# A fused attention and expert kernel: the round's products in pieces of 32 weight columns, and another order of two transfers and a store

## What is computed

```python
q, k, v = split_heads(x @ Wq), split_heads(x @ Wk), split_heads(x @ Wv)      # 16 heads of 8
attn = softmax(einsum('bhqd,bhkd->bhqk', q, k) * e ** -0.5) + bias[None]
x = _layernorm(x + _layernorm_eps3(einsum('bhqk,bhkd->bhqd', attn, v)) * gamma + beta)
sim = (x @ hasher_w.T) @ keys.T
vals, idx = top_k(sim, 4); w = softmax(vals)
for k in range(4):
    out += (silu(x @ values_down[idx[k]]) @ values_up[idx[k]]) * w[k]
x = _layernorm(x + (x + out * scale))
```

## Time and profile before

| | us |
|---|---|
| median of 3 runs | 327.17 |
| lowest and highest | 325.89, 327.17 |
| the profiled execution's own time | 326.0 |
| its span in the profile | 324.2 |

### The profile page before, as it was taken

How to read it: one execution, slowest core, us unless ns; L and a number is a source line. 1 busy time by engine, 2 the same in 40 slices (tenths; PEclk the granted TensorE clock), 3 DMA queues, 4 the chain that set the end, 5 groups by cost and what they waited for, 6 DMA issues and landing times.

```text
span 324.2 us, 4925 instructions
## 1 busy us (share of the span) xinstructions
PE 296.1 (91%) x1633; PEld 125.3 (39%) x1658; DVE 233.2 (72%) x516; ACT 200.5 (62%) x392; POOL 125.7 (39%) x209
## 2 busy tenths in 40 slices
PE   4778979999999989999999999996999999999991
PEld 2544322223232233333544533332455433275481
DVE  4548778788879869987778699873876763156673
ACT  3675366685767567788655577884646689911610
POOL 8492700110104641146466111493275022963133
PEclk9999999999999999999999999997999999999998
DMA  5486593279520203020202020024000000100002
GB/s 164 109 248 162 132 328 88 62 273 305 156 74 4 74 2 77 2 73 4 73 4 73 4 74 3 1 66 116 0 4 0 4 3 1 34 0 2 0 0 65
DMA packets 28246, 23.17 MB, mean 71 GB/s; under 512 B 6542, under 2 KB 26686, under 8 KB 28222
## 3 DMA queue, kind: packets, MB, share of 16 engines
q1 hardware_dynamic: 27950, 22.73, 24.7%
q10 hardware_dynamic: 272, 0.13, 0.1%
HBM read 12.18 MB, written 10.52 MB: 70 GB/s over the span
## 4 chain that ended last, share of the span: by engine, by line
PE 71%; DVE 10%; ACT 6%; DMA 4%; POOL 3%; issue 3%; SPq 1%; POOLq 0%; DVEq 0%
PE sm_ps L1136 18%; PE ov_ps L1165 16%; PE st_ps L1147 12%; DVE neg_max L830 6%; PE si_ps L1183 6%; PE mi_ps L1259 5%; ACT probs L705 3%; PE mi_ps L1171 2%; PE st_ps L1388 2%; DMA q_stack<-shift_rows 2%; DMA k_stack<-stack_dram 1%; PE si_ps L1189 1%; PE mi_ps L1244 1%; PE si_ps L1264 1%; PE st_ps L1189 1%
## 5 line engine op out<-in xcount | busy, mean ns | idle before, releaser
L830 DVE TENSOR_REDUCE neg_max<-sm_ps 128x1 f32<-128x512 f32 x256 | 167.3, 686 | 48.7 <-PE sm_ps L1136 47.5
L705 ACT ACTIVATE probs<-st_ps 128x512 f32<-128x512 f32 x256 | 137.5, 606 | 47.2 <-PE st_ps L1147 39.4
L1136 PE MATMUL sm_ps<-k_stack,q_stack 96*128 96x512 bf16 x256 | 98.5, 386 | 5.7 <-DVE neg_max L830 2.4
L1147 PE MATMUL st_ps<-q_stack,k_stack 128*128 128x512 bf16 x232 | 78.5, 382 | 3.9 <-DMA q_stack<-shift_rows 2.5
L1165 PE MATMUL ov_ps<-probs,v_cur 128*32 128x512 f32 x512 | 69.1, 611 | 0.0
L1136 PEld LDWEIGHTS sm_ps<-k_stack,q_stack 96*128 96x128 bf16 x256 | 24.7, 97 | 94.4 <-DVE neg_max L830 76.3
L472 POOL TENSOR_TENSOR hid<-hid,w_rows 128x512 f32<-128x512 f32 x26 | 32.7, 1274 | 38.3 <-ACT w_rows L616 38.2
L1147 PEld LDWEIGHTS st_ps<-q_stack,k_stack 128*128 128x128 bf16 x256 | 25.0, 99 | 29.7 <-ACT probs L705 8.2
L893 DVE SCALAR_TENSOR_TENSOR hid<-tanh_sb,mi_ps 128x512 f32<-128x512 f32 x24 | 16.3, 681 | 12.3 <-ACT tanh_sb L742 12.3
L1259 PE MATMUL mi_ps<-x_t,down_sb 128*128 128x512 f32 x48 | 24.5, 591 | 0.2 <-ACT probs L705 0.2
L1183 PE MATMUL si_ps<-up_sb,hid 128*128 128x128 f32 x192 | 24.3, 275 | 0.0
(11 more groups left out here) (162 smaller groups left out, 296.8 us busy)
## 6 DMA issues: line engine op xcount, KB each, us to landing
stack_dram<-parts SPq DMA_DIRECT2D x18, 384.0 KB, 4.5
q_stack<-stack_dram SPq DMA_DIRECT2D x16, 288.0 KB
k_stack<-stack_dram SPq DMA_DIRECT2D x16, 288.0 KB
stack_dram<-parts SPq DMA_DIRECT2D x6, 288.0 KB, 4.4
x_sb<-L_attn_x SPq DMA_DIRECT2D x4, 256.0 KB, 3.2
out<-y_out SPq DMA_DIRECT2D x3, 256.0 KB, 2.3
stack_dram<-parts SPq DMA_DIRECT2D x6, 96.0 KB, 2.1
down_sb<-L_ffn_values_down SPq DMA_DIRECT2D x1, 512.0 KB, 8.2
```

The costliest lines, as they stand in the source:

```text
L705: nc.scalar.activation(probs[:, u % 2, j, :], st_ps[:, score_bank(u * J + j), :], ACT.Exp, scale=SCORE_SCALE).then_inc(probs_ready, 1)
L830: nc.vector.tensor_reduce(neg_max[:, g % 2, col:col + 1], sm_ps[:, c % 2, :], AX.X, ALU.max, negate=True).then_inc(max_ready, 1)
L1136: nc.tensor.matmul(sm_ps[:, c % 2, :], q_stack[0:SHIFT_ROW, h, c * P:(c + 1) * P], k_stack[0:SHIFT_ROW, h, :], start=True, stop=True).then ...
L1147: nc.tensor.matmul(st_ps[:, score_bank(k), :], k_stack[:, g * J + j, kc * P:(kc + 1) * P], q_stack[:, g * J + j, :], start=True, stop=True ...
```

## The change

`tiled` makes one product as separate matmuls, each with 32 of the weight columns and the whole moving operand, into the quarters of 32 partitions of the same bank; `tiled_turn` does the same for a bf16 transpose, `whole` is the product as it was. Scores, maxima, both expert layers, `sim`, the spreads, and the bf16 turns (`shift`, `wt`) of the rounds go through them. Whole as before are: the set-up, the maxima made in it, the f32 transposes (`o0`, `o1`, `x1t`), and in the tail the spreads, the first layer and the last `up`. The tail's eight `up` of the sequence before the last use the same function `up` as the rounds, and so are in pieces too. In SyncE's queue `load_shift(t + 1, 0)` now stands ahead of `load_slice(t + 1, 2)`, and `store(t - 2)` behind both. The rest of the diff gives names to places and tables that hold the same places as before.

```diff
--- before.py
+++ after.py
@@ -393,14 +401,14 @@
                     load_slice(t + 1, 1)
                 if attention:
                     load_shift(t, 3)
-                if late:
-                    store(t - 2)
                 if is0(t):
                     for b in range(3, B):
                         write_parts(b, slice(0, H), parts_written[b])
                 if attention and more:
+                    load_shift(t + 1, 0)
                     load_slice(t + 1, 2)
-                    load_shift(t + 1, 0)
+                if late:
+                    store(t - 2)
 
             def store(f):
 
@@ -1124,7 +1133,23 @@
                                          wv_sb[:], start=True, stop=True)
                 i.then_inc(prep_mm, 1)
 
-            def maximum_scores(t, pos, c):
+            def tiled(dst, weights, moving, **flags):
+
+                for n in range(weights.shape[-1] // TILE):
+                    i = nc.tensor.matmul(dst[n * TILE:(n + 1) * TILE], weights[:, n * TILE:(n + 1) * TILE], moving,
+                                         **flags)
+                return i
+
+            def tiled_turn(dst, src, idn):
+
+                for n in range(src.shape[-1] // TILE):
+                    i = nc.tensor.transpose(dst[n * TILE:(n + 1) * TILE], src[:, n * TILE:(n + 1) * TILE], idn)
+                return i
+
+            def whole(dst, weights, moving, **flags):
+                return nc.tensor.matmul(dst, weights, moving, **flags)
+
+            def maximum_scores(t, pos, c, product=tiled):
 
                 n, h = t * U + pos, pos % U
                 k = C * n + c
@@ -1133,8 +1158,8 @@
                 if not (is0(t) and pos == 0 and c < 2):
 
                     pe.wait_ge(max_ready, k - 1)
-                nc.tensor.matmul(sm_ps[:, c % 2, :], q_stack[0:SHIFT_ROW, h, c * P:(c + 1) * P],
-                                 k_stack[0:SHIFT_ROW, h, :], start=True, stop=True).then_inc(sm_ready, 1)
+                product(sm_ps[:, c % 2, :], q_stack[0:SHIFT_ROW, h, c * P:(c + 1) * P], k_stack[0:SHIFT_ROW, h, :],
+                        start=True, stop=True).then_inc(sm_ready, 1)
 
             def scores(t, u, j):
 
@@ -1144,9 +1169,8 @@
                 if not (is0(t) and k < 3):
 
                     pe.wait_ge(probs_ready, J * n + j + 1 - scores_since(k))
-                nc.tensor.matmul(st_ps[:, score_bank(k), :],
-                                 k_stack[:, g * J + j, kc * P:(kc + 1) * P],
-                                 q_stack[:, g * J + j, :], start=True, stop=True).then_inc(scores_ready, 1)
+                tiled(st_ps[:, score_bank(k), :], k_stack[:, g * J + j, kc * P:(kc + 1) * P],
+                      q_stack[:, g * J + j, :], start=True, stop=True).then_inc(scores_ready, 1)
 
             def values(t, u):
 
@@ -1180,8 +1204,8 @@
                         pe.wait_ge(side_done, count)
                 pe.wait_ge(weighed, hidden_count(f, j))
                 for c in range(C):
-                    i = nc.tensor.matmul(si_ps[:, c * P:(c + 1) * P], hid[:, j, c * P:(c + 1) * P], up_sb[:, j, :],
-                                         start=(j == 0 and c == 0), stop=(j == FJ - 1), skip_group_check=True)
+                    i = tiled(si_ps[:, c * P:(c + 1) * P], hid[:, j, c * P:(c + 1) * P], up_sb[:, j, :],
+                              start=(j == 0 and c == 0), stop=(j == FJ - 1), skip_group_check=True)
                 if j == FJ - 1:
                     i.then_inc(side_ready, 1)
 
@@ -1229,7 +1253,7 @@
                 elif name.startswith("shift"):
                     g = int(name[5:])
                     pe.wait_ge(shift_split, (t + 1 if g == 0 else t) * G + g + 1)
-                    i = turn(mi_bf[:, 0:P], shift_parts[:].rearrange("p i n -> p (i n)"), ident_bf[:])
+                    i = tiled_turn(mi_bf[:, 0:P], shift_parts[:].rearrange("p i n -> p (i n)"), ident_bf[:])
                 elif name == "x1t":
                     if t < B:
                         pe.wait_ge(pool_step, pool_at(f, "bscale"))
@@ -1241,14 +1265,14 @@
 
                     pe.wait_ge(misc_done, job(t, "x1t", is_kept))
                     for c in range(C):
-                        i = nc.tensor.matmul(bank[:, c * NE:(c + 1) * NE], x1_t[:, c * P:(c + 1) * P], sim_w[:],
-                                             start=True, stop=True)
+                        i = tiled(bank[:, c * NE:(c + 1) * NE], x1_t[:, c * P:(c + 1) * P], sim_w[:],
+                                  start=True, stop=True)
                 elif name == "wt":
                     pe.wait_ge(w_split, f + 1)
                     pe.wait_ge(spread_made, PARTS)
                     for c in range(C):
-                        i = turn(si_bf[0:PARTS * NE, c * P:(c + 1) * P], w_parts[:, c].rearrange("p i n -> p (i n)"),
-                                 ident_bf[:])
+                        i = tiled_turn(si_bf[0:PARTS * NE, c * P:(c + 1) * P],
+                                       w_parts[:, c].rearrange("p i n -> p (i n)"), ident_bf[:])
                 elif name in SPREAD:
                     pe.wait_ge(side_done, job(t, "wt", is_side))
                     i = spread_weights(bank[:, :], int(name[1:]))
@@ -1256,12 +1280,12 @@
                     j = int(name[4:])
                     if j == 0:
                         pe.wait_ge(experts_loaded, 32)
-                    i = nc.tensor.matmul(mi_ps[:], down_sb[:, j * NJ:(j + 1) * NJ, :], x1_t[:],
-                                         start=True, stop=True)
+                    i = tiled(mi_ps[:], down_sb[:, j * NJ:(j + 1) * NJ, :].rearrange("k n d -> k (n d)"), x1_t[:],
+                              start=True, stop=True)
                 i.then_inc(ready, 1)
 
-            def spread_weights(bank, j):
-                return nc.tensor.matmul(bank, spread[:, j].rearrange("r n p -> r (n p)"), w_t[:], start=True, stop=True)
+            def spread_weights(bank, j, product=tiled):
+                return product(bank, spread[:, j].rearrange("r n p -> r (n p)"), w_t[:], start=True, stop=True)
 
             early = [divmod(k, C) for k in range(EARLY)]
 
@@ -1269,7 +1293,7 @@
 
                 for _ in range(n):
                     if early and EARLY - len(early) < most:
-                        maximum_scores(0, *early.pop(0))
+                        maximum_scores(0, *early.pop(0), product=whole)
 
             for b in range(B):
                 prep(b)
@@ -1382,7 +1406,7 @@
                     nc.tensor.matmul(bank, ident_bf[:], k_stack[:, 0, :], start=True, stop=True)
 
             def tail_spreading(j):
-                spread_weights(tail_bank(j), j).then_inc(tail_spread, 1)
+                spread_weights(tail_bank(j), j, product=whole).then_inc(tail_spread, 1)
 
             def tail_first_layer(j):
                 nc.tensor.matmul(tail_down_bank(j), down_sb[:, j * NJ:(j + 1) * NJ, :], x1_t[:],
```

## The result

| | before | after |
|---|---|---|
| median us | 327.17 (4 runs) | 312.98 (4 runs) |
| lowest and highest | 325.89, 327.39 | 312.77, 313.24 |
| profiled execution, its span | 326.0, 324.2 | 312.77, 311.0 |

The ratio is 0.9574, 95% interval 0.9549 to 0.9600: faster by 14 us by the medians, by 13.2 between the two profiled executions. 324.2 was forecast. The time lies at rival 1 (311.7), which had a chance of 0.20; the range held it.

A forecast was written before the change was run, and what follows sets the result against it. TensorE was taken to bound most of rounds 2 and 3, ScalarE the last window. Queue -4.3 and shape +2.5 sum to -1.8 us, from the profiled 326.0 to 324.2 us; range 311.5 to 335.

The forecast's parts named there:

- rival 1: Tiles cost nothing over a whole product: a plain unit takes 2.64 instead of 2.85; 311.7 us in all, chance 0.20.
- What bounds the kernel: TensorE in round 2 and first half of round 3, ScalarE in the last window, a two-engine loop in round 0.
- Part 1, the queue: End of round 2: shift rows issued ahead of slice and store close the 2.7 us hole and its low clock, -4.3 us.
- Part 2: The shape, 32-column pieces in rounds and tail: -2.6 + 2.2 + 1.5 + 1.4 = +2.5 us.
- Price of a product of 32-column weights: A product in 32-column pieces takes 0.24 us instead of 0.22, so a plain unit changes by -0.03.
- A smaller step: In round 2, small transposes and `sim` together were to cost 0.3 us.
- Rival 3: Four times the pairs make instructions the bound, 0.06 us a pair, in rounds and tail: +11.8, 338 us, chance 0.20.
- The rule weighed: Each further tile adds about 4 ns: a product would take 0.23, the shape about 3 us less in rounds 1 to 3.

## Why the prediction was wrong

- **What bounds the kernel: right.** TensorE in most of the rounds, VectorE in round 0, ScalarE at the end of round 3, a hole of 2.7 us with its low clock.
- **Part 1, the queue: right.** -4.3 forecast; -4.2 by the spans of the queue-alone run, 4.3 by its round 2. That it is worth 6.2 once the shape is changed was not seen: the forecast simply added the two.
- **Part 2, the failing step: "Price of a product of 32-column weights", 0.24 instead of 0.22.** It measures 0.22. The 0.02 came from the values' second pass, 0.45 behind the first instead of 0.43. That pass stood right behind a change of shape, and the excess is a part of it: with the same shape ahead, the values step 0.43. The prediction asked whether the excess was special to f32, and not whether it was special to the place behind a change. The one misread row went into a plain unit twice: as 8 x 0.02 lost by the products in pieces, and as 2 x 0.02 that the values' two passes were not expected to get back. These 0.20 us are the difference between the forecast -0.03 a unit and the measured -0.23.
- **What hangs on that step.** Round 0: -2.6 forecast, -2.6 measured, and that is luck. The forecast had each of 16 units go from 3.09 to 2.93. In the trace 13 units lose 0.21 to 0.22 (3.09 becomes 2.87, rival 1's figure), two stay, and the one with the f32 transposes, which stay whole, is 0.18 longer. Round 1: 0, measured -2.0. Round 2, shape alone: +2.2, measured 62.7 - 69.2 + 4.3 = -2.2. Round 3: +1.5, measured -1.6. Tail: +1.4, measured -0.3: its 256 pairs of `up` take 7.20 us, row below, against 7.31. Rounds and tail together, the shape is worth about -8.7 on top of the queue's -4.3; +2.5 was forecast.
- **A smaller step.** `sim` was forecast to cost (in the 0.3 for small transposes and sim) and took 0.5 us less each time, up to 2 us in all.
- **Rival 1: right, and nearly in size.** -3.5, -2.6, -2.8, -1.3 by rounds; measured -2.6, -2.0, -2.2, -1.6. It gave rounds 0 and 1 too much, since it let every unit gain, and in part of them something else than TensorE sets the pace. That its total of -14.3 is so near the 13.2 has some luck in it: it had neither the 1.9 us by which queue and shape help each other nor what `sim` saves.
- **Rival 3, instructions as the bound: wrong.** It needed 0.033 us a pair in the tail; measured are 0.027, after TensorE's timeline in the tail:

```profile
273.49 7.20 PE L1139 MATMUL si_ps<-up_sb,hid 128*32 128x128 f32 x256
```

  (7.20 - 0.27) / 255 = 0.027, held for 7 us; the 32 pairs of `sim` behind it go at 0.012 each (284.52 to 284.91, rows in the last section). It was priced from one instruction behind an idle stretch; the burst of eight in the same rows, 0.16 us, was the better witness.
- **The rule weighed.** The Trainium skill ("TensorE: Matmul & The Clock Gate", Part 3, The mechanism) has about 4 ns for each further tile. From the first to the fourth start within a score it is 10 ns in the median of the kernel after, 3 to 4 ns each, so the figure fits, but it isn't paid per product: each quarter is started again 0.22 us after its last start, and the step from product to product stays at 0.22. Behind a change of shape, as at the values before, it is 20 ns. Two starts this close also lie well under the 25 ns between starts that the prediction set beside rival 3. The same page of the Trainium skill, section "Wait — 56ns, not 53.3ns?", has about 62 ns of sequencer time for a matmul without the hardware decode; an estimate by it for the tail's 256 matmuls is 15.9 us, and the row above has 7.20, so that path was not the one taken.

What stays open is what the 0.10 us of a change consists of. The traces show that loads aren't made ahead over it, and that the next product's first load starts some 0.10 us after the 0.22 of the product ahead (158.17 to 158.49 above); whether that is a drain of the array, a part of the load, or both, was not varied by itself. Open too is what `sim` in pieces is worth by itself.

## What to carry to other kernels

Count the changes of tile shape between neighbouring products, not the instructions: each costs 0.10 us or more, so one small product of another shape in every unit is paid 64 times, and it can pay to cut everything else to its shape. Do it for all or for none: with two thirds or one third of the products cut, this kernel was slower than with none. And when a price is read from a row, ask what stands ahead of that row; an excess right behind a change may belong to the change.

## What the runs showed of the hardware that was not expected

- Four 32-column products side by side start 3 to 4 ns apart and take together 0.22 us for 512 columns each, the same as one 128-column product, wherever they stand back to back in the rounds. Two of 64 columns do so as well, but 0.24 right behind a change.
- One pair of changes of shape costs 0.20 us at a bf16 product of 512 columns, 0.23 at an f32 one, 0.32 at an f32 one of 128 columns, where the second pass is late by another 0.10; eight small bf16 turns that alternate in shape take 1.31 us, where the same work in one shape takes 0.22.
- `sim` (four f32 products of 32 moving columns) takes 0.39 us in pieces to the next product in the tail, against 0.88 whole. Whole, its eight passes step 0.11, as long as those of `up` with four times the moving columns, so it isn't the moving columns that set the pace. That it was the load of 128 f32 columns (0.19 us, one started every 0.11) is argued. Before, then after:

```profile
297.32 1.05 PE L1244 MATMUL mi_ps<-sim_w,x_t 128*128 128x32 f32 x8
298.20 1.96 PE L1388 MATMUL st_ps<-x_t,down_sb 128*128 128x512 f32 x4
```

```profile
284.52 0.46 PE L1139 MATMUL mi_ps<-sim_w,x_t 128*32 128x32 f32 x32
284.91 2.84 PE L1412 MATMUL st_ps<-x_t,down_sb 128*128 128x512 f32 x6
```

- A pair of load and matmul every 27 ns held for 7 us in the tail, and in the scores and maxima of the run with eight pairs a product; that run's instruction queue moved 47 packets instead of 13 before, without a visible wait.
- After a stop of 3.3 us the granted clock stood at 0.50 for 6 us, after one of 2.7 us at 0.55 in the mean of 3.8 us; one execution each.
